# Decoder layer on one core: the first normalisation moves to ScalarE, u moves up in VectorE's order, and GpSimd's order in a step changes

## The reference

```python
conv[n] = c * conv[n-1] + x[n]                        # complex; the real part is used
x1 = layernorm(x + conv.real * x)                     # u = (1 + conv.real) * x
q, k, v = relu(x1 @ Wq + bq), relu(ctx @ Wk + bk), relu(ctx @ Wv + bv)
out = softmax(q k^T / 4) v + q                        # 16 heads of 16 channels
x2 = layernorm(x1 + layernorm(out) * ln_g + ln_b)
xn = rms_norm(x2); ids = argmin(dist2(xn, centroids)) # one of 8 experts for each token
y = (a * silu(g)) @ down_w[ids],  a, g = split(xn @ up_w[ids])
return layernorm(2 * x2 + y)
```

## Time and profile before

| | us |
|---|---|
| median of 3 runs | 1281.18 |
| lowest, highest | 1277.73, 1294.08 |
| the profiled execution's own time | 1285.39 |
| its span | 1283.3 |
| busy in the span: PE, DVE, POOL, ACT | 1114.9, 953.8, 792.0, 664.2 |

### The profile page before, as it was taken

How to read it: one execution, slowest core, us unless ns; L and a number is a source line. 1 busy time by engine, 2 the same in 40 slices (tenths; PEclk the granted TensorE clock), 3 DMA queues, 4 the chain that set the end, 5 groups by cost and what they waited for, 6 DMA issues and landing times. The chain is left out here.

```text
span 1283.3 us, 27523 instructions
## 1 busy us (share of the span) xinstructions
PE 1114.9 (87%) x8060; PEld 817.8 (64%) x8061; DVE 953.8 (74%) x2411; ACT 664.2 (52%) x1413; POOL 792.0 (62%) x943
## 2 busy tenths in 40 slices
PE   0599999999999998999999999830999999999996
PEld 0465666666666666666666666520788888888885
DVE  6357799899899899899899898639455555555553
ACT  1247577676677677776776677514322222222221
POOL 6545778888788888888887865344133333333333
PEclk9859899999899999999999999755999999999998
DMA  5556755655556646656556555206011111111110
GB/s 143 131 158 173 189 144 143 154 138 150 141 142 149 160 130 153 151 146 155 142 146 152 141 134 128 76 25 180 25 53 49 44 52 49 52 46 47 53 49 22
DMA packets 90827, 144.92 MB, mean 113 GB/s; under 512 B 12663, under 2 KB 78336, under 8 KB 84513
## 3 DMA queue, kind: packets, MB, share of 16 engines
q1 hardware_dynamic: 84192, 126.61, 38.3%
q0 software_dynamic: 6528, 16.99, 4.5%
HBM read 91.44 MB, written 53.03 MB: 113 GB/s over the span
## 5 line engine op out<-in xcount | busy, mean ns | idle before, releaser
L888 DVE TENSOR_REDUCE neg_max_sb<-S 128x2 f32<-128x512 f32 x512 | 327.9, 682 | 78.6 <-PE S L693 77.6
L559 ACT ACTIVATE probs<-T 128x512 f32<-128x512 f32 x512 | 278.5, 595 | 152.4 <-PE T L706 140.5
L693 PE MATMUL S<-k_st,q_st 48*128 48x256 f32 x1024 | 215.4, 320 | 51.5 <-DMA k_st<-k_pieces 26.0
L693 PEld LDWEIGHTS S<-k_st,q_st 48*128 48x128 f32 x1024 | 146.7, 193 | 131.1 <-issue 56.3
L706 PE MATMUL T<-q_st,k_st 49*128 49x256 f32 x1024 | 210.5, 318 | 3.7 <-ACT probs L559 2.1
L706 PEld LDWEIGHTS T<-q_st,k_st 49*128 49x128 f32 x1024 | 145.6, 192 | 21.0 <-ACT probs L559 16.2
L1201 ACT ACTIVATE gT<-GT 128x512 f32<-128x512 f32 x71 | 42.6, 600 | 207.5 <-PE GT L1236 207.5
L669 PE MATMUL O<-probs,v_aug 128*32 128x256 f32 x2048 | 147.1, 408 | 0.7 <-ACT probs L559 0.7
L1177 POOL DMA_INDIRECT out<-res,token x71 | 76.4, 1076 | 101.5 <-DVE res L1309 101.5
L1258 PE MATMUL Y<-dn_sb,gT 128*128 x568 | 134.2, 379 | 0.8 <-ACT gT L1201 0.8
L513 POOL DMA_INDIRECT buckets<-row,slot x64 | 66.2, 1034 | 90.4 <-DVE slot L1052 80.2
(11 more groups left out here) (177 smaller groups left out, 2551.6 us busy)
## 6 DMA issues: line engine op xcount, KB each, us to landing
q_st<-q_pieces SPq DMA_DIRECT2D x64, 256.0 KB, 4.7
k_st<-k_pieces SPq DMA_DIRECT2D x64, 256.0 KB, 5.9
xr<-buckets SPq DMA_DIRECT2D x71, 129.0 KB, 2.1
xt<-in_x SPq DMA_DIRECT2D x32, 256.0 KB, 6.4
ct<-in_ctx SPq DMA_DIRECT2D x32, 256.0 KB, 6.8
up_sb<-in_L_ffn_up_w SPq DMA_DIRECT2D x8, 1024.0 KB, 8.6
q_pieces<-q_hi SPq DMA_DIRECT2D x32, 256.0 KB, 2.1
q_pieces<-q_lo SPq DMA_DIRECT2D x32, 256.0 KB, 2.1
```

The source lines that it names most:

```text
L559: a_.activation(probs[:, h % 8].rearrange("p k t -> p (k t)"), T_ps[h % 2][:, :], ACT.Exp, scale=DH ** -0.5).then_inc(s["exp_ok"], 1)
L693: last = t_.matmul(S_ps[h % 2][:, c * TOK:(c + 1) * TOK], q_st[base:base + STACK, h, c * P:(c + 1) * P], k_st[base:base + STACK, h, :], st ...
L888: v.tensor_reduce(neg_max[:, cur.mod(2), :, h], S_ps[h % 2][:, :].rearrange("p (c t) -> p c t", c=NTC), AX.X, ALU.max, negate=True).then_i ...
```

## The change

On DVE, `u` moves from `h` = 3 to `h` = 0, right behind maxima 0 and 1 and ahead of `row`; its statistics and moments stand together at `h` = 2. x1 = (u - mean) * rstd leaves DVE's `h` = 13 and is computed on ACT at `h` = 13, behind v, as Identity(u * rstd + shift), one instruction for each of the two halves of the tokens; DVE makes shift = -mean * rstd (128x2) at `h` = 10. ACT takes over the waits for `shift` and for y2 of four sequences before. On POOL the cut of k comes before `conv_imag` 0 and `conv_input` before the scatter.

```diff
@@ POOL step
+                    cut(n, k32[:, :, :], k_hi, k_lo, "k_ok", "k_cut", k_out)
                     conv_imag(t + 3, 0)
-                    cut(n, k32[:, :, :], k_hi, k_lo, "k_ok", "k_cut", k_out)
                     conv_imag(t + 3, 1)
                     rstd(a, "lnx", 4, mvx, rsx, "rstdx")
+                    conv_input(t + 3)
                     if active(b):
...
-                    conv_input(t + 3)
                     rstd(a, "ln2", 4, mv2, rs2, "rstd2")
@@ ACT step
+                        if h == 13 and active(n + 1):
+                            nn = n + 1
+                            wait(act, "shift", nn)
+                            wait(act, "y_ok", nn - 4, 4)
+                            for c in range(NTC):
+                                a_.activation(x1[:, nn.mod(4), c], u[:, c], ACT.Identity, bias=shift[:, c:c + 1],
+                                              scale=rs1[:, 1, c:c + 1]).then_inc(s["x1_ok"], 1)
@@ DVE step
+                        if h == 0 and active(nn):
+
+                            wait(dve, "x1_ok", nn - 1, 2)
+                            wait(dve, "conv", nn, 5)
+                            wait_ring(dve, x_in[nn.mod(2)], nn, 2, 16)
+                            v.scalar_tensor_tensor(u[:, :, :], state[:, 0], 1.0, xt[:, nn.mod(2)], ALU.add, ALU.mult).then_inc(s["u_ok"], 1)
                         if h == 0 and active(b):
...
-                        if h == 3 and active(nn):
-
-                            wait(dve, "x1_ok", nn - 1, 2)
-                            wait(dve, "conv", nn, 5)
-                            wait_ring(dve, x_in[nn.mod(2)], nn, 2, 16)
-                            v.scalar_tensor_tensor(u[:, :, :], state[:, 0], 1.0, xt[:, nn.mod(2)], ALU.add, ALU.mult).then_inc(s["u_ok"], 1)
-                        if h == 4 and active(nn):
+                        if h == 2 and active(nn):
                             wait(dve, "u_ok", nn)
                             wait(dve, "rstd1", nn - 1, 2)
                             stats(nn, u, st1, "ln1")
+                            moments(nn, st1, mv1, "ln1")
                         if h == 5:
                             if active(a):
                                 divide(a, 0, 0)
-                            if active(nn):
-                                moments(nn, st1, mv1, "ln1")
-                            if active(a):
                                 divide(a, 0, 1)
...
+                        if h == 10 and active(nn):
+                            wait(dve, "rstd1", nn, 2)
+                            v.scalar_tensor_tensor(shift[:, :], mv1[:, :, 0], -1.0, rs1[:, 1], ALU.mult, ALU.mult).then_inc(s["shift"], 1)
...
-                        if h == 13 and active(nn):
-                            wait(dve, "rstd1", nn, 2)
-                            wait(dve, "y_ok", nn - 4, 4)
-                            for c in range(NTC):
-                                v.tensor_scalar(x1[:, nn.mod(4), c], u[:, c], mv1[:, c, 0:1], rs1[:, 1, c:c + 1],
-                                                ALU.subtract, ALU.mult).then_inc(s["x1_ok"], 1)
```

More of the change, by code:

```diff
@@ L143, in build @@
             rs1 = sb1("rs1", [P, 2, NTC])
+            shift = sb1("shift", [P, NTC])
             x1 = sb1("x1", [P, 4, NTC, C])
@@ L202, in build @@
                 negT neg_ok neg_out neg_in0 neg_in1 t_pe exp_ok pv o_ev x_pe o_ok qn_pe qn_ok oq_ok lnx rstdx
-                x1b_ok y_ok ln2 rstd2 x2_ok rms xw_ok offset nx_ok xnT_pe xnT_ok dist_pe pick rank_pe slot_ok
+                x1b_ok y_ok ln2 rstd2 x2_ok rms xw_ok offset shift nx_ok xnT_pe xnT_ok dist_pe pick rank_pe slot_ok
                 id_ok scat0 scat1 pool_waits sp_waits dve_waits"""
```

## The result

Slower: 1305.9 us against 1287.2 in medians of four executions each, on the same chip; the ratio is 1.0147 (95% interval 1.0093 to 1.02). The forecast was 1283, two above the median before; the kernel lost 19. The profiled execution took 1296.91 around a span of 1295.0, against 1285.39 and 1283.3; it was the fastest of its four.

The account below looks back on a forecast made before the run. It took the loop from x1's transpose through DVE and ACT's tail as bound: 0.59 x 22.85 + 0.41 x 24.75 = 23.63, plus 0.2 for the clock, 23.83 against 23.76, +2 us over 25 steps: 1283 us, range 1252 to 1306.

Parts of the forecast that it names:

- u behind maxima 0 and 1: On DVE, `u` escapes POOL's long product and costs 0.68 us instead of up to 2.52; little of it is path.
- 1.1 us stall: PE's stall of about 1.1 us for maxima 6 in steps with the long `u`; said to go.
- cut ahead of conv_imag 0: On POOL, cut starts 0.9 us earlier; PE's 1.10 us `k_st` stall falls to about 0.2; second `oq` ends 0.3 later.
- y2 blocked by conv_input: On DVE, y2, due at 416.1, is locked out by POOL's conv_input until 416.45 and ends at 417.3.
- clean step: Step in which onehot isn't caught by POOL's lock; forecast 22.85 us, 0.59 of the steps.
- x1 on ACT: Two Identity on ACT take 0.84 us, bounds 0.7 and 1.2, and wait for y2; ACT's tail then ends at 420.2.
- The loop: Transpose of x1, S6, DVE from maxima 6 to y2, ACT's tail to the ctT copy: the expected bound.
- rival A: The forecast itself: gains eaten by locks on `oq`, gain and y2 and by ACT's tail; within 12 us; chance 0.45.
- The caught step: Step where POOL's lock delays onehot, then conv_input blocks the first gain: 24.75 us, 41% of steps.
- rival B: The lock collisions on DVE don't occur: 1263 us, or 1252 if y2 is free too; chance 0.32.
- clock term: On PE, +0.2 us a step for the granted clock, scaled from 0.97 on the third of the loop on PE.

Follow-up runs that it names:

- s3: The kernel before with only the early `u` and its statistics and moments moved; ratio to before 1.0021 [0.9993, 1.005].
- s1: The kernel before with only the cut of k moved ahead of `conv_imag` 0; ratio to before 1.0014 [0.9975, 1.0054].
- e3: The changed kernel with five places for x1 instead of four (`place` shares the memory of `cand`); 1271.2 us, ratio to before 0.9894.
- g2: e3 with onehot written as two tensor_scalars instead of one instruction with two SBUF inputs; ratio to before 1.0038 [1.0007, 1.0068].
- e4: The changed kernel with five needless matmuls in PE's stalls at the step's end, around the transposes of x1; ratio to before 1.0015 [0.9985, 1.0046].
- g1: The changed kernel with five needless matmuls inside PE's stretch, ahead of the transposes of o at `h` = 5; ratio to before 1.0633.
- e1: The changed kernel with x1 back on DVE behind y2, without shift; 1316.6 us, ratio to before 1.0257 [1.0184, 1.033].
- e2: The changed kernel with `conv_input` back behind the scatter; ratio to before 1.0067 [1.0017, 1.0116].
- g4: The changed kernel with onehot written as two tensor_scalars instead of one instruction with two SBUF inputs; ratio to before 1.045 [1.0386, 1.0513].
- s2: The kernel before with only `conv_input` moved ahead of the scatter; ratio to before 1.0053 [1.001, 1.0097].
- h1: e3 with onehot in its old form moved behind the statistics and moments of `oq`, at `h` = 9; 1255.5 us, ratio to before 0.9777.

## Why the prediction was wrong, step by step

**u behind maxima 0 and 1**: right. 681 ns, the lower bound. That it is no path by itself held too (s3: 1.0021). The 1.1 us stall that was to go with it was put in the wrong place: the rows of before have it ahead of S0 at the step's end (299.49 above), and PE's wait for the maxima stayed at 10.9 us in all, in shorter pieces (22 times, 0.8 at most, for 16 and 1.1).

**cut ahead of conv_imag 0**: right. The k_st wait fell from 10.1 to 1.5 us. The price on `oq` is right as well: 1057 ns against 896, and there are two in a step, 0.32 us. Alone, s1 kept 7.7 us of the wait, so in the whole change something else took the rest away; the shift of the step is the likely one, not shown.

**y2 blocked by conv_input**: wrong, by little. Forecast: issued at 416.1, held until 416.45. Measured in the clean step: conv_input from 316.98 to 318.25 and y2 at 318.26, back to back and 0.87 us long. Whether that is a lock or chance can't be read from one row; y2's mean of 471 ns says that it was never held for long. 

**x1 on ACT**: forecast 0.84 for the pair, measured 1.09 (593 ns each). The nearest row by shape, a pair of Relu out of PSUM, was too low by 0.25; the bound of 1.2 was nearer. It made up for y2: y2 ended 0.37 us earlier in the step than forecast, ACT's tail took 3.1 us behind it instead of 2.9, and the clean step came out at 22.75 for 22.85. That it is so near is in part luck, two misses of opposite sign. The loop (rival A's mechanism) is shown, by the wait for ctT and by e3, which takes it away and gains 2.5% against after.

**The caught step**: 24.75 forecast, 24.64 measured, with the onehot under the operation L424 that follows the cut, and the gain under conv_input, as said. Timelines of POOL, DVE and PE of after in the step from 371.0:

```profile
384.13 1.70 POOL L424 TENSOR_TENSOR state<-state,decay 128x512 f32<-128x512 f32 x1
384.60 1.26 DVE L1035 TENSOR_TENSOR onehot_bf<-expert_no,choice 128x16 bf16<-128x16 f32 x1
...
388.11 1.27 POOL L434 TENSOR_TENSOR state<-state,xt 128x512 f32<-128x512 f32 x1
388.17 1.50 DVE L1007 SCALAR_TENSOR_TENSOR o<-oq,mvx,g_bc 128x256 f32<-128x256 f32 x1
...
395.62 0.63 PE L657 MATMUL M<-ident,x 128*128 128x128 f32 x4 [0.56 <-ACT ctT L581]
```

The share was wrong: 41% was taken over from before, and 5 of 26 steps (19%) were caught. Half way to rival B, then, and by the sum of the forecast (0.81 x 22.85 + 0.19 x 24.75 = 23.2) a gain of 0.5 us a step. Both lengths and the Trainium skill, "SBUF — State Buffer", section "SBUF: two separate sides", agree with a port that is taken for a whole instruction; its wording also covers g2, since a VectorE operation in one of the fast modes takes part in the lock even with one input in SBUF. Which of the modes onehot ran in, no row here shows.

**The failed step is the clock term.** The sum added +0.2 us a step for the granted clock, scaled from the 0.97 of the earlier trace rows, as if the clock of before were a property of the chip that the new step would inherit. It is a consequence of where PE stands. The falls cost about 1.0 us a step in after (26 us over 26 steps) and 0.2 to 0.6 in before, by the two prices above, where they are already inside the 23.76. 23.2 for the work and 1.0 for the falls is the 24.2 measured. The forecast had named PE's stall for ctT as what would show the loop, and had not asked what PE's stalls at the step's end do to the clock. The size fits the profiled pair: the step came out 0.39 us over the forecast's 23.83, over 25 steps 10 us, and 1296.91 stands against the 1287 forecast for the profiled execution. The other 13 us of the median's miss lie outside the sum: this execution was 9 us under the median of its four, at their highest clock, and the profiled one of before 4 us over the median of its three. That stalls at this place do it is shown by e4 against g1. That they come as a pair is not what does it (e1, e2). That the clock is what took the time back is shown by e2 and e4: both end under after, though their clean or caught steps (23.27, 23.90) are longer than its clean ones.

What stays open: how often the clock falls, and so why after has twice the falls of before. It isn't PE's idle time over the whole step: in the 590 us windows e2 leaves PE idle 2.1 us a step and after 1.6, with two falls and 14. Where PE stands at the step's end orders the kernels better, but not fully. The usual sum of its stalls in the last 4 us before the transposes of x1, with the falls: e4 0 us, none; e3 0.58, four; g2 0.96, none; e2 1.01, two; before 1.08, seven; after and g1 1.14, 14 and 15; g4 1.07 or 1.37, 16; e1 1.57, 17. Beside it stands a rival that no run tests: the length of the step. The kernels whose steps are nearly all 23.9 us (e2, g2) have few falls or none, and those with steps of 22.75 (after), 24.9 (g1) and 24.7 (g4) have many; no run changed the length and left the stalls alone. Open as well: why the early `conv_input` alone lowers the clock (in s2's profile PE stands 1.2 or 1.5 us at most steps' ends, 1.08 before), why POOL takes the port between `oq` and onehot in one step and not in the next, and 6 of the 19 us.

## What to carry to other kernels

Ask of a change that shortens DVE's or ACT's work where PE will stand instead, and what the clock does behind it: here the steps without a fall became 0.4 us shorter and the falls took back 0.7 us a step. When one buffer ties an early producer to a late reader, one place more in the ring (e3, 2.5% against after) can be worth more than an order of the work around the tie. And a short operation of DVE between two long ones is best put behind those that don't meet POOL (h1), not rewritten.

## What the runs showed of the hardware beyond the forecast

- 11 of the 14 stretches at half clock in after lasted 3.4 us and three 6.8; one of 3.4 costs some 1.55 us of a step of 22.75, as DVE and ACT wait too. The 14 in 26 steps came with PE busy 93% of the time (551.40 of 590 us). In all kernels nearly all of them began within 2.5 us of the transposes of x1, where PE had just stood. The Trainium skill, "TensorE: Matmul & The Clock Gate", Part 1, section "The HAM clock gate", tells of two levels, and the trace agrees: 0.50 from 323 to 326 us. Its table of the two ties the lower one to an idle engine; this one was busy in all but 7% of the time and stood 1.14 us in two pieces before it fell.
- Work added can be time gained: five matmuls that compute nothing, put into the stalls, made the kernel 1.3% faster than after (e4); the same five elsewhere made it 4.8% slower (g1), 2.2 us a step for the five.
- A POOL operation that waits gets in between two DVE operations that follow each other without a gap: in the rows from 384.13 L424, issued while `oq` runs until 384.68, takes 1.70 us (1.27 for the same operation in the earlier trace rows), and onehot behind it 1.26 where it takes 0.19 in another step. It is caught in 5 to all 26 of 26 steps depending on what stands around it, and once in 28 when moved (h1). One input less didn't free it.
- An Identity of 128x256 with a scale and a bias per partition, out of SBUF, takes 593 ns on ACT (L620 above).
